# Attention scores from two float32r parts in 24 rows instead of three bfloat16 parts in 56 rows, and another order of issue on PE

## What is computed

```
x = x + layernorm(attention(layernorm(x)))   # 16 heads, logits = q k^T / sqrt(8) + bias[head, i - j]
                                             # bias from exp(-sharpness * (offset - rel)^2); softmax over 1024 keys
x = x + layernorm(ffn(layernorm(x)))         # inside: x + msa(ln(x)), plain softmax, w_qkv and w_proj;
                                             # then x + mixture of 8 experts (argmax gate, gelu), one expert a token
```

## Time and profile before

| | |
|---|---|
| median of three runs | 986.7 us |
| the profiled execution's own time | 982.59 us |
| its span in the trace | 980.9 us |
| stage 0, from its first to its last first-pass or second-pass matmul | about 52 to 478 us |
| stage 1, the same | about 532 to 851 us |
| PE matmuls busy | 830.7 us |
| DVE busy | 750.7 us |
| ACT busy | 648.3 us |

### The profile page before, as it was taken

The page is one execution under the profiler, slowest core; times in us unless marked ns, Lnnn a source line. Parts: engine busy times, 40 slices in busy tenths (PEclk is TensorE's granted clock), DMA queues, the critical chain, the costliest instruction groups (busy, mean ns, idle before and its releaser), DMA issues.

```text
span 980.9 us, 22683 instructions
## 1 busy us (share of the span) xinstructions
PE 830.7 (85%) x9011; PEld 315.4 (32%) x9011; DVE 750.7 (77%) x1211; ACT 648.3 (66%) x1272; POOL 136.7 (14%) x376
## 2 busy tenths in 40 slices
PE   2449999999999999999735799999999999974770
PEld 1203333333333333333312122222222222354760
DVE  6477777777777777774297899999999999266544
ACT  5406777677777777777434499999999999710222
POOL 8100000000000000000010011011010110003772
PEclk9758999999999999999967599999999999975995
DMA  2654434444444443330005365322222121010123
GB/s 62 173 157 104 120 95 109 105 106 107 107 98 110 107 106 93 87 86 16 16 1 152 81 149 134 105 69 70 65 66 70 58 69 42 24 44 19 50 49 94
DMA packets 55609, 82.79 MB, mean 84 GB/s; under 512 B 12336, under 2 KB 42480, under 8 KB 55504
## 3 DMA queue, kind: packets, MB, share of 16 engines
q1 hardware_dynamic: 53648, 76.57, 29.6%
q0 software_dynamic: 1472, 3.02, 1.3%
q10 hardware_dynamic: 384, 1.76, 0.6%
HBM read 62.31 MB, written 19.01 MB: 83 GB/s over the span
## 4 chain that ended last, share of the span: by engine, by line
PE 65%; ACT 9%; DVE 7%; POOL 4%; issue 4%; DMA 2%; SPq 1%; DVEq 0%; POOLq 0%
PE bank L1155 22%; PE bank L1200 17%; PE bank L1207 14%; PE bank L1147 8%; ACT prob_mem L737 8%; POOL moe_out L653 2%; POOL prob_mem L642 2%; DVE stats L796 1%; DVE norm L810 1%; DVE unit_max L879 1%; PE bank L1362 1%; DMA prob_mem<-tokens,gather_u 1%; DVE meanvar L799 1%; PE bank L1372 1%; DMA k_parts<-prob_mem 0%
## 5 line engine op out<-in xcount | busy, mean ns | idle before, releaser
L737 ACT ACTIVATE prob_mem<-bank 128x512 f32<-128x512 f32 x1024 | 556.1, 597 | 137.8 <-PE bank L1207 120.3
L876 DVE CUSTOM_DVE_ANT_0 y_res<-bank,tables 128x1024 bf16<-128x1024 f32 x256 | 312.3, 1224 | 99.5 <-PE bank L1147 94.3
L1155 PE MATMUL bank<-prob_mem,v_ring 128*32 128x256 f32 x4096 | 320.2, 387 | 4.6 <-issue 2.6
L879 DVE TENSOR_REDUCE unit_max<-bank 128x1 f32<-128x1024 f32 x256 | 293.2, 1216 | 13.8 <-PE bank L1147 10.7
L1147 PE MATMUL bank<-k_rows,q_rows 56*128 56x512 bf16 x512 | 161.2, 418 | 44.6 <-DMA k_rows<-k_parts 30.2
L1200 PE MATMUL bank<-q_rows,k_rows 59*128 59x512 bf16 x512 | 164.2, 391 | 2.3 <-ACT prob_mem L737 0.7
L1200 PE MATMUL bank<-more_rows 59*128 59x512 bf16 x512 | 158.9, 383 | 3.1 <-ACT prob_mem L737 1.1
L1147 PE MATMUL bank<-more_rows 56*128 56x512 bf16 x512 | 159.0, 382 | 0.0
L1207 PE MATMUL bank<-feat,flip 96*32 96x512 bf16 x2048 | 158.8, 387 | 0.0
L1155 PEld LDWEIGHTS bank<-prob_mem,v_ring 128*32 128x32 f32 x4096 | 102.2, 109 | 159.8 <-ACT prob_mem L737 72.9
L598 POOL CAST max_parts<-unit_max 128x8 bf16<-128x8 f32 x64 | 12.1, 189 | 689.7 <-DVE unit_max L876 386.1
(11 more groups left out here) (160 smaller groups left out, 571.5 us busy)
## 6 DMA issues: line engine op xcount, KB each, us to landing
tables<-bias_rows SPq DMA_DIRECT2D x30, 480.0 KB, 5.3
unit_sums<-o_ring SPq DMA_DIRECT2D x64, 128.0 KB, 1.7
more_rows<-q_parts SPq DMA_DIRECT2D x64, 96.0 KB
more_rows<-k_parts SPq DMA_DIRECT2D x32, 192.0 KB
q_rows<-q_parts SPq DMA_DIRECT2D x56, 96.0 KB
k_rows<-k_parts SPq DMA_DIRECT2D x28, 192.0 KB
feat<-bias_parts SPq DMA_DIRECT2D x14, 378.0 KB, 3.8
w_moe<-in_L_ffn_w_dram SPq DMA_DIRECT2D x16, 256.0 KB, 3.8
```

What stands on the lines that cost most here:

```text
L737: nc.scalar.activation(prob[:, kb, half * N:(half + 1) * N], b_bank(entry(ul, kb, half)), ACT.Exp).then_inc(exp_done[a], 1)
L876: nc.vector.tensor_tensor_reduce(out=no_use[qb % 2], in0=scores, in1=bias, scale=1.0, scalar=LEAST, op0=ALU.add, op1=ALU.max, accum_out=un ...
L879: nc.vector.tensor_reduce(unit_max[:, slot, qb:qb + 1], scores, AX.X, ALU.max).then_inc(max_done[1], 1)
L1155: ins = nc.tensor.matmul(AV[VM * c:VM * (c + 1), :], v_ring[:, head_slot, b * QB + kb, :], prob[:, kb, c * W:(c + 1) * W], start=(kb == 0) ...
```

## The change

- q and k are kept as two float32r parts: ACT makes the first (rounded by writing it as float32r), DVE the remainder. The second bfloat16 cast on ACT and the second subtraction on DVE are gone. q k^T becomes the sum of three products of parts, 24 rows, 26 with the maxima, which are split in two parts by two POOL operations instead of four.
- The rows stand in one tensor `ring` of four head slots: partitions 0 to 23 and 32 to 55 hold the first pass's operands of half 0 and 1, partitions 64 and 96 on those of the second pass. So the four matmuls of a step go to the four quarters of the array's rows. The moving operand's rows are kept only for the half that they serve (`T / 2` columns).
- A head takes 18 DMAs instead of 10 (16 where one sequence is loaded), in float32; the parts are stored with one DMA for q and one for k, of 2 x 4 bytes a value instead of 3 x 2.
- PE issues both first-pass halves first, then waits for a bank, second-pass half 0, waits, second-pass half 1.
- The transposition of the maxima is in float32. `tables` now shares memory with the experts' weights, and two small tensors of the routing move into `prob_mem`; one POOL memset of 64 partitions x 4 x 2048 float32 takes the place of four of 32 partitions x 4096 bfloat16.

```diff
-    KR = 7 * DH
-    QK_DMAS = 10
+    KR = 3 * DH
+    RG = P // 4
+    QK_DMAS = 16 + 2
...
-                    sp.wait_ge(part_lo[a], 2 * g + 1)
-                    sp.dma_start(qp_dram[a][:, :, :, cols].rearrange("h d t n -> (h d) t n"),
-                                 parts[:, 0, :, cols]).then_inc(parts_stored[a], 16)
-                    sp.wait_ge(part_lo[a], 2 * g + 2)
-                    for t in range(3):
-                        sp.dma_start(kp_dram[a][:, t, :, cols], parts[:, 1, t, cols]).then_inc(parts_stored[a], 16)
+                    for s in range(2):
+                        sp.wait_ge(part_lo[a], 2 * g + s + 1)
+                        sp.dma_start((qp_dram, kp_dram)[s][a][:, :, :, cols].rearrange("h d t n -> (h d) t n"),
+                                     parts[:, s, :, cols]).then_inc(parts_stored[a], 16)
...
+                        for whole in (True, False):
+                            at = (2 * (s if whole else 1 - s) + f) * RG
+                            if whole:
+                                cols, off, inner = slice(b0 * L, b1 * L), b0 * L, [[1, (b1 - b0) * L]]
+                            else:
+                                cols, off, inner = slice(T + b0 * N, T + b1 * N), b0 * L + f * N, [[L, b1 - b0], [1, N]]
+                            twice = [[2 * T, DH], [0, 2]] if s == 0 else [[T, 2 * DH]]
+                            last = T if s == 0 else 0
+                            if whole or s:
+                                sp.dma_start(ring[at:at + 2 * DH, slot, cols],
+                                             bass.AP(head.tensor, head.offset + off, twice + inner)).then_inc(loaded, 16)
+                            else:
+                                for b in range(b0, b1):
+                                    sp.dma_start(ring[at:at + 2 * DH, slot, T + b * N:T + (b + 1) * N],
+                                                 bass.AP(head.tensor, head.offset + b * L + f * N, twice + [[1, N]])).then_inc(loaded, 16)
+                            sp.dma_start(ring[at + 2 * DH:at + KR, slot, cols],
+                                         bass.AP(head.tensor, head.offset + last + off, [[2 * T, DH]] + inner)).then_inc(loaded, 16)
...
-                    for s in range(2):
-                        act.wait_ge(part_rest[a], 2 * g + s + 1)
-                        nc.scalar.copy(parts[:, s, 1, cols], rest[:, g % 2, s, :]).then_inc(part_mid[a], 1)
...
-                rows = slice(f * HP, f * HP + KR)
-                return nc.tensor.matmul(SA[slot][:, f, :], q_ring[head_slot][rows, b * L + qb * P:b * L + (qb + 1) * P],
-                                        k_ring[head_slot][rows, b * L + f * N:b * L + (f + 1) * N], start=True, stop=True)
+                rows = slice(f * RG, f * RG + KR)
+                return nc.tensor.matmul(SA[slot][:, f, :], ring_r[rows, head_slot, b * L + qb * P:b * L + (qb + 1) * P],
+                                        ring_r[rows, head_slot, T + b * N:T + (b + 1) * N], start=True, stop=True)
...
-                rows = slice(f * HP, f * HP + KR + 3)
+                rows = slice((2 + f) * RG, (2 + f) * RG + KR + 2)
...
+                            if not done:
+                                block_a(a, u + AU, lu, kb, True).then_inc(sa_done[a], 1)
                             for f in range(2):
                                 b_bank_free(a, i, entry(ul, kb, f), first, last)
                                 ins = scores_b(a, ul, kb, f)
                                 if a == 1:
                                     ins.then_inc(sb_done[1], 1)
-                                if not done:
-                                    ins = block_a(a, u + AU, lu, kb, f == 0, (1 - f,))
-                            if not done:
-                                ins.then_inc(sa_done[a], 1)
```

119 lines of the change are left out of this document (46 added, 73 removed).

## The result

The changed kernel takes 1117.35 us in the median of four runs. They fall into two pairs, 1055.69 and 1059.51 us at a mean granted clock of 0.86, and 1175.19 and 1176.14 at 0.72; this split is the subject of most of what follows. The faster pair against before's 986.89 gives a ratio of 1.072, 95% interval 1.068 to 1.076. Forecast were 986 us and a range of 969 to 1006: it is slower than before by 69 us at best and by 189 at worst.

What follows compares the result with a forecast made beforehand. PE was taken to bound stage 0, with the ring of three banks close by, and DVE stage 1. Terms -11 + 11 - 1.5 + 1 = -0.5 on a median of 986.7 gave 986 us, range 969 to 1006.

Steps and rivals of the forecast that it cites:

- The bound of stage 0: Stage 0: PE bounds it at 1.52 us a step without a gap; without the second pair PE alone needs 1.29.
- the ring of three banks: Stage 0: second half waits for the previous exponential to free its bank; limits a unit to 11.85 us, from 12.54.
- The stream: Score matmuls: 512 float32r columns cost between bfloat16's 0.21 us and float32's 0.43; float32r was expected not to stream like float32.
- Rival 1: Score matmuls: float32r streams at two cycles a column; stage 0 +43 us, about 1040 us in all; chance 15%.
- The load: Stage 0's ring: extra exposed weight load 0.04 us a step, between 0 and 0.10; 0.32 us a unit.
- Rival 2: Stage 0's ring: the weight load is exposed in full at 0.10 us; about 1000 us in all; chance 15%.
- Stage 0's gain of 11 us: Stage 0: gain of (0.69 - 0.32) x 30 = 11 us over the 30 units with a first pass.
- the first steps of both stages: Start of each stage at half clock: the missing pair is worth twice as much; -1.5 us (0 to -3).
- The starts: Both stage starts: more row DMAs on SP's queue delay the maxima store 5.5 us each; +11 us (4 to 20).
- What PE saves in stage 1 isn't worth anything: Stage 1: DVE is the bound at 1.16 us a block, ACT and PE close behind; no gain from PE's saving.
- fifth rival: Whole kernel: the clock falls because PE would stream less; no size and no chance given.
- the term of +1: Stage 1: later `weigh_v` and next step (0 to +4) and maxima queued behind row DMAs; +1 us together.

Runs made afterwards that it cites:

- experiment 2: The changed kernel with its parts stored and multiplied in bfloat16, same rows, quarters, order and number of transfers; 983.94 us, ratio 1.0033 to before.
- experiment 1: The changed kernel with both halves of each pass on the same quarter of the rows, so one stream follows the other; 1629.57 us.
- experiments 4 to 13: Matmuls added, weighting halved, or starts filled or relieved, in the changed kernel (1073.65 to 1269.85 us) or its bfloat16-parts version (weighting halved 1010.51, float32r fillers 1230.74).
- 4: The changed kernel with each first-pass matmul of stage 1 issued twice; 1269.85 us, ratio 1.297.
- experiment 5: The changed kernel with one extra bfloat16 matmul on 24 rows ahead of each first-pass matmul of stage 1, overwritten; 1232.62 us.
- 14: The kernel of experiment 2 with the k side's rows of the first two heads issued on ACT's queue at both starts; 971.23 us, ratio 0.9854 to before.
- 15: The kernel of 14 with the experts' weights loaded in units 8 to 15 of stage 1 instead of 0 to 7; 967.39 us, ratio 0.9808 to before.
- experiment 8: The changed kernel without half of the weighting of v in stage 1 (key blocks 1, 2, 4 and 5 of each unit); 1121.46 us.
- experiment 13: The kernel of experiment 2 without half of the weighting of v in stage 1 (key blocks 1, 2, 4 and 5 of each unit); 1010.51 us.
- 11: The changed kernel with one bfloat16 matmul of 128 rows and 512 columns ahead of each block's first pass in stage 1, overwritten; 1073.65 us.
- experiment 9: The changed kernel with bfloat16 matmuls on the full array filling PE's waits at the start of stage 1; 1088.29 us.

## Why the prediction was wrong, by its own steps

**The bound of stage 0** was right. The second pair's time goes, the ring of three banks is next, and with a load of the old length the unit is 11.85 us (experiment 2).

**The stream** was right. That it costs what a bfloat16 stream does was the author's assumption, which no run had shown; experiment 1 shows it, with 0.60 us from pair to pair at 0.50, where twice the bfloat16 stream would be 0.82. Rival 1 is out.

**The load** was mis-sized. Taken 0.04 us a step between ends of 0 and 0.10; it is 0.106 (experiment 2). No run shows the 0.04, which was the author's estimate; the row that told the truth was the float32 load of 128 columns with 190 ns against 93. In this ring the second half's load starts only behind the wait for the exponential (at 203.65 us in the changed kernel, with 0.21 us of waiting recorded on it), so the whole difference of the records counts, 0.09 of the 0.106. Rival 2 held for this term. The float32 transposition, taken with about 0.05 us more, is recorded with 0.28 us for 0.22 in bfloat16. Stage 0's gain of 11 us became a loss: with 12.70 for 12.54 it is 0.16 x 30 = 5 us, the last two units, at 12.7 for 11.85 and 12.35, are 1.2 more, every eighth unit is 13.68 for 13.33, and the rest of the 10.7 is in the first units. For the first steps of both stages the prediction had -1.5 at half clock; here they cost about 4 more, and the clock reached 1.00 only 14.2 us behind the first second pass where it took 6.9 before (91.5 and 79.8 us). The four-byte load is recorded with 0.18 us for 0.09, and what it adds to a step, 0.106, is more than twice the estimate.

**The starts** were half right. Taken 5.5 us each, +11 with 4 to 20. Stage 0's is +4.4: from first first-pass to first second-pass matmul +7.9, of which the earlier stores gave back 3.5. Stage 1's is +12.0: +2.8 to the first first-pass matmul and +9.2 from there. Together 16.4. The number of issues was right, the 0.39 us for each wasn't: sixteen take 548.27 - 540.55 = 7.72 us, 0.48 each, since issues that read each source row twice take 0.66 to 0.72, the next shape 0.46 and the k side 0.31. Nor is SP's queue all of it. The first maxima's copy ends at 568.26 and their store goes out at 573.59, 5.3 us later, where before it went out 0.03 us behind the copy. That much is the queue. The other 3.9 of the 9.2 come before the copy: PE waits 6.4 us for the second sequence's rows, for 3.3 before, a landing that the prediction priced at +1 and set off against -1 for the first stores.

```profile
540.55 0.72 SPq L394 DMA_DIRECT2D ring<-q_parts  x1
541.31 0.46 SPq L400 DMA_DIRECT2D ring<-q_parts  x1
...
547.96 0.31 SPq L400 DMA_DIRECT2D ring<-k_parts  x1
...
555.56 0.70 SPq L394 DMA_DIRECT2D ring<-q_parts  x1
...
573.59 0.31 SPq L424 DMA_DIRECT2D maxima_rows<-max_rows  x1
```

The copy of the first maxima, before and after:

```profile
546.14 0.25 ACT L724 COPY max_rows<-bank 24x128 bf16<-24x128 bf16 x1 [19.80 <-PE bank L1184]
```

```profile
568.00 0.26 ACT L716 COPY max_rows<-bank 16x128 f32<-16x128 f32 x1 [26.10 <-PE bank L1170]
```

**Stage 1** is where the step failed that cost most. "What PE saves in stage 1 isn't worth anything" held for the clock that before had. The prediction named the fall of the clock as a fifth rival, and neither its sum nor its chances have anything for it. The row of before for the clock with less work on PE, 1.00 from 461 to 464 us, in units without a first pass, is of stage 0, where each step also has the bias matmuls on 96 rows beside the weighting on 128. Stage 1 has no bias, and its scores went from 56 and 59 rows to 24 and 26. That this is why the clock falls there is argued from experiments 4 to 13, and isn't shown outright; that it falls, and what it costs, is. So that row has another mixture of work than stage 1, and doesn't speak for it. At 1.00 the term of +1 is about right in kind: 9.44 for 9.26 a unit, near 4 us over the units there. At 0.50 a unit costs 14.23, 5 us more, and stage 1 lost 40.6 us in the profiled execution. There is no profile of the two executions near 1176. The 31 units between the first and the last copy of sums took 328.7 us (595.3 to 924.0); all of them at 14.23 would be 441, 112 more, an estimate of 1168 us, near their 1176, and their mean clock of 0.72 to 0.73 is near the 0.71 of experiments 4 and 5, which stayed at 0.50 in all of stage 1.

**Direction and size.** Without the clock's fall the measured terms are +10.7 for stage 0, +16.4 for the starts and +5 for stage 1 (0.18 x 28 units): 982.6 + 32 = 1015 us, and 1020 with the +5.4 behind stage 1, which weren't looked into. The load and the starts alone, 982.6 + 27 = 1010, would have put the time just outside of the range, and the term that was left out, the clock in stage 1, makes up the other 36 us to 1055.69.

Experiment 2 shows the same from the other side: without the longer load and with the clock up, the kernel is 0.3% slower than before. Its trace has stage 0 13.3 us shorter, from first second-pass matmul to last exponential (392.3 for 405.6): the 0.69 us a unit of the prediction's ring are there, but the second unit takes 17.4 us for 12.5. The start of stage 0 isn't longer (-2.5); that of stage 1 is by 5.2, and stage 1 itself by 9.8 (309.6 for 299.7), all of it in the first ten units, where PE waits 4.4, 6.3, 1.1 and 3.0 us for the maxima rows and the clock falls beside three of these waits; the later units are shorter than before's, 9.05 for 9.26. The prediction had +1 for these queues. With the starts cut (14, 15) 14 to 19 us of gain appear.

## What to carry to other kernels

Before a change takes rows of the array or streams out of PE's work, read the granted clock in each stage and ask what in that very stage streams over all rows; here a stage that DVE bounded at 1.00 with 9.44 us a unit fell to 0.50 from 655 to 702 us, and there PE bounded it with 14.23. PE busy without a gap is no sign of health (20.00 of 20 us at 0.50 here): look at the clock column beside it. In the ring of stage 0 the wait made the weight load visible in full, 0.09 of 0.106 us a step, so compare load records of the same shape, and price DMA issues by their shape (0.31 to 0.72 us each here), not by their number.

## What the runs showed of the hardware

- Granted clock and work: with PE busy without a gap from 600 to 1080 us the clock stayed at 0.50 (experiment 5). With 128-row work taken away, the float32r kernel was at 0.50 in nearly all of stage 1, mean clock 0.74 (experiment 8; 0.86 and 0.72 in the changed kernel's two pairs), and the bfloat16 kernel's mean fell from 0.91 to 0.80 (experiment 13). Falls came beside waits of PE (2.23 us at 653 in the changed kernel, 4.4, 6.3 and 3.0 in experiment 2, 2.4 and 3.9 in 11), another without a long one (584 us in experiment 9, with 0.48 us the longest wait); gaps alone don't account for these runs. In experiment 13 PE also stood still more, so that run doesn't separate the two.
- Whether and when the clock rises differs between executions of one program: 1056 us at a mean clock of 0.86 and 1176 at 0.72 for the changed kernel.
- float32r: at 0.50 a second pair of 512-column streams starts 0.60 us behind the first, load included (experiment 1), where bfloat16 has 0.41; weights of 128 columns 0.18 us at 1.00 where bfloat16 has 0.09.
- SP's issues at the start of stage 1 in the changed kernel, the sixteen from 540.55 us on: of a DMA that reads each source row twice 0.66 to 0.72 us, of plain rows 0.46 on the q side and 0.31 or 0.32 on the k side.
